# A graph layer on one core: the preamble's loads and searches in another order

## The reference

```python
h_self  = x @ W_self.T + b_self
messages = x[src] @ W_neigh.T + b_neigh
h_neigh = segment_sum(messages, dst, num_segments=50000)
out = layernorm(x + relu(h_self + h_neigh))      # over the 128 features, eps 1e-5
```

## Time and profile before

| | us |
|---|---|
| median of three runs | 803.71 (801.73 to 805.24) |
| profiled execution | 807.21 |
| its span, from the first to the last instruction | 805.3 |
| busy: PE, DVE, POOL, ACT | 548.5, 446.5, 405.0, 303.8 |

### The profile page before, as it was taken

One profiled execution on the slowest core, in us unless ns is written; L12 is line 12 of the kernel. 1 busy time (PEld: TensorE's weight loads), 2 busy tenths in 40 slices (PEclk: granted clock), 3 DMA queues, 4 the chain that ended last, 5 costly groups with the idle time before them and its releaser, 6 DMA issues.

```text
span 805.3 us, 11397 instructions
## 1 busy us (share of the span) xinstructions
PE 548.5 (68%) x3151; PEld 434.5 (54%) x3151; DVE 446.5 (55%) x1927; ACT 303.8 (38%) x789; POOL 405.0 (50%) x424
## 2 busy tenths in 40 slices
PE   1036020118941879889678787888989798999995
PEld 0024010016730657677456576666767576778784
DVE  6783001008821768689566666675645455666765
ACT  0000000015501444446244354435445354566566
POOL 3687777731176556562756566556656566200000
PEclk9999555558985799999879999889979899999998
DMA  4222222113331435444334444434544444433333
GB/s 136 62 63 65 53 52 62 52 27 92 102 83 52 113 103 145 125 129 128 93 93 132 119 122 110 126 110 132 133 110 129 129 126 129 122 109 101 112 107 93
DMA packets 122933, 82.12 MB, mean 102 GB/s; under 512 B 15374, under 2 KB 115894, under 8 KB 122840
## 3 DMA queue, kind: packets, MB, share of 16 engines
q1 hardware_dynamic: 109208, 53.63, 23.5%
q0 software_dynamic: 13664, 27.77, 13.6%
HBM read 55.44 MB, written 26.71 MB: 102 GB/s over the span
## 4 chain that ended last, share of the span: by engine, by line
PE 41%; issue 21%; DVE 15%; another core or an unknown queue 11%; ACT 6%; POOL 4%; DMA 2%; ACTq 1%; DVEq 0%; POOLq 0%
PE bank L889 17%; PE bank L908 8%; PE bank L909 7%; DVE pick L724 4%; PE bank L873 4%; ACT result L1017 3%; PE bank L904 3%; DVE y L735 2%; PE bank L883 2%; DVE stats L755 2%; ACT sums_t L990 1%; POOL ring L462 1%; DMA dst_block<-in_dst,block_index 1%; POOL dst_block L422 1%
## 5 line engine op out<-in xcount | busy, mean ns | idle before, releaser
L462 POOL DMA_INDIRECT ring<-in_x,chunk_src x391 | 379.9, 972 | 265.7 <-issue 110.2
L990 ACT COPY sums_t<-bank 128x496 f32 x131 | 74.9, 572 | 415.5 <-remote 223.1
L889 PE MATMUL bank<-pick,ring 128*128 128x192 f32 (+2 forms) x782 | 227.6, 431 | 2.4 <-DMA ring<-in_x,chunk_src 2.4
L908 PE MATMUL bank<-wsum_t,x_t 128*128 128x128 f32 (+1 forms) x782 | 173.2, 304 | 11.7 <-issue 11.5
L735 DVE SCALAR_TENSOR_TENSOR y<-bank,x_in 128x384 f32<-128x384 f32 x131 | 72.5, 554 | 191.5 <-PE bank L909 73.9
L909 PE MATMUL bank<-wn_t,sums_t 128*128 128x128 f32 (+1 forms) x782 | 158.6, 284 | 19.4 <-issue 19.4
L1017 ACT ACTIVATE result<-y,minus_mean,rstd 128x128 f32<-128x128 f32 x391 | 163.4, 486 | 0.0
L889 PEld LDWEIGHTS bank<-pick,ring 128*128 128x128 f32 x782 | 142.5, 205 | 17.1 <-DMA ring<-in_x,chunk_src 1.9
L908 PEld LDWEIGHTS bank<-wsum_t,x_t 128*128 128x128 f32 (+1 forms) x782 | 124.8, 200 | 37.7 <-issue 37.7
L909 PEld LDWEIGHTS bank<-wn_t,sums_t 128*128 128x128 f32 (+1 forms) x782 | 125.5, 201 | 18.9 <-issue 18.9
L724 DVE TENSOR_SCALAR pick<-columns,local 128x192 f32<-128x192 f32 (+2 forms) x391 | 118.0, 357 | 0.2
(11 more groups left out here) (122 smaller groups left out, 208.8 us busy)
## 6 DMA issues: line engine op xcount, KB each, us to landing
x_in<-in_x SPq DMA_DIRECT2D x130, 192.0 KB
out<-result SPq DMA_DIRECT2D x130, 192.0 KB
ring<-in_x,chunk_src POOLq DMA_INDIRECT x391
degrees_t<-degrees_dram SPq DMA_DIRECT2D x130, 2.2 KB
dst_padded<-in_dst SPq DMA_DIRECT2D x1, 390.6 KB
src_padded<-in_src SPq DMA_DIRECT2D x1, 390.6 KB
edge_src<-in_src SPq DMA_DIRECT2D x1, 390.6 KB
edge_dst<-in_dst SPq DMA_DIRECT2D x1, 390.6 KB
```

The lines of the kernel that those rows point to most:

```text
L462: nc.gpsimd.indirect_dma_start(ring[:, c % RING, :], None, x, bass.IndirectOffsetOnAxis(ap=chunk_src[:, c:c + 1], axis=0)).then_inc(gather ...
L889: ins = mm(sums[:, lo:hi], ring[:, c % RING, :], pick[tau % DEEP][:, PICK_AT[q]:PICK_AT[q] + hi - lo], start=(tau == 0 and q == 0), stop=( ...
L908: mm(h, x_t[b][:, q, 0:rows], k.wsum_t[:], start=False, stop=False)
L990: nc.scalar.copy(sums_t[:, bass.ds(at, SPAN)], sum_bank[tau % SUM_BANKS][:, 0:SPAN]).then_inc(sums_placed, 1)
```

## The change

SP: the four first `x` loads go behind the bias loads, and the bias loads wait for the windows of column 0. The three loads of the edge list for the check move into the main loop, to the step that loads `x` tile trio 37. POOL: all four `dst` blocks of the ranks and the first tile block are fetched before the windows of column 0, the other tile blocks after them; the windows of columns 1 to 3 now go before the tile windows. DVE: the search for tile blocks goes before the search in the first rank block, the last bias parts and the search in rank blocks 1 to 3 go before the packing, and only the tile search is left inside it. Nothing is added to or taken from what is computed, except the wait on `window_landed[0]` on SP.

```diff
--- before.py
+++ after.py
@@ -365,32 +365,36 @@  (sync engine)
+            def load_edges():
+
+                sp.dma_start(edge_src[:], src.rearrange("(p e) -> p e", p=EDGE_ROWS)).then_inc(edges_landed, 16)
+                sp.dma_start(edge_dst[:, 0:EDGE_COLS], dst.rearrange("(p e) -> p e", p=EDGE_ROWS)).then_inc(edges_landed, 16)
+                sp.wait_ge(next_set, 1)
+                sp.dma_start(edge_dst[0:EDGE_ROWS - 1, EDGE_COLS:EDGE_COLS + 1],
+                             dst.rearrange("(p e) -> p e", p=EDGE_ROWS)[1:EDGE_ROWS, 0:1],
+                             allow_slow_non_contiguous=True).then_inc(next_landed, 16)
+
...
-            for tau in range(DEEP):
-                load_x(tau)
-
-            sp.dma_start(edge_src[:], ...
-            sp.dma_start(edge_dst[:, 0:EDGE_COLS], ...
-            sp.wait_ge(next_set, 1)
-            sp.dma_start(edge_dst[0:EDGE_ROWS - 1, EDGE_COLS:EDGE_COLS + 1], ...
-
             sp.wait_ge(k.parts_made, 3)
+            sp.wait_ge(window_landed[0], 32)
             for q in range(TRIO):
                 sp.dma_start(k.bias[q * PARTS:(q + 1) * PARTS, q, :], ...
 
+            for tau in range(DEEP):
+                load_x(tau)
             store_degrees(1, 0, 1)
...
                 if tau == FIRST_TRIOS:
                     store_degrees(2, 1, 2)
+                if tau == FIRST_TRIOS + DEEP:
+                    load_edges()
@@ -440,17 +444,18 @@  (gpsimd)
             pool.wait_ge(blocks_found, 1)
             load_blocks(0, [0])
+            pool.wait_ge(blocks_found, 2)
+            load_blocks(0, range(1, COLUMNS))
+            pool.wait_ge(blocks_found, 3)
+            load_blocks(1, [0])
             pool.wait_ge(padded_stored, 64)
             pool.wait_ge(places_found, 1)
             load_windows([0])
-            pool.wait_ge(blocks_found, 2)
-            load_blocks(0, range(1, COLUMNS))
-            pool.wait_ge(blocks_found, 3)
-            load_blocks(1, range(COLUMNS))
+            load_blocks(1, range(1, COLUMNS))
             pool.wait_ge(places_found, 2)
+            load_windows(range(1, COLUMNS))
+            pool.wait_ge(places_found, 3)
             load_tile_windows(range(COLUMNS))
-            pool.wait_ge(places_found, 3)
-            load_windows(range(1, COLUMNS))
@@ -540,9 +545,9 @@  (vector engine)
             find_blocks(0, 0, 1)
             find_blocks(0, 1, COLUMNS)
-            find_rank_places(0, 1)
             dve.wait_ge(ends_spread, 2)
             find_blocks(1, 0, COLUMNS)
+            find_rank_places(0, 1)
@@ -641,31 +646,30 @@
             v.tensor_copy(k.bias_part[:, 0, :, :], k.bias_row[:]).then_inc(k.parts_made, 1)
 
-            pack_start(0, 1)
-            pack_bits(0, 1, range(0, 3))
-            find_tile_places(0, COLUMNS)
-            pack_bits(0, 1, range(3, 5))
-            find_rank_places(1, COLUMNS)
-            pack_bits(0, 1, range(5, SHIFT_BITS))
-            pack_end(0, 1)
...
-            take_lists(1, 0, 1)
-            spread_lists(1, 0, FIRST_TRIOS, 0, FIRST_TRIOS - 1)
-
             dve.wait_ge(k.parts_made, 1)
             link(v.tensor_tensor(k.bias_rest[:, 0, :, :], k.bias_row[:], k.bias_part[:, 0, :, :], ALU.subtract))
             v.tensor_copy(k.bias_part[:, 1, :, :], k.bias_rest[:, 0, :, :]).then_inc(k.parts_made, 1)
             dve.wait_ge(k.parts_made, 2)
             link(v.tensor_tensor(k.bias_rest[:, 1, :, :], k.bias_rest[:, 0, :, :], k.bias_part[:, 1, :, :], ALU.subtract))
             v.tensor_copy(k.bias_part[:, 2, :, :], k.bias_rest[:, 1, :, :]).then_inc(k.parts_made, 1)
+            find_rank_places(1, COLUMNS)
+
+            pack_start(0, 1)
+            pack_bits(0, 1, range(0, 3))
+            find_tile_places(0, COLUMNS)
+            pack_bits(0, 1, range(3, SHIFT_BITS))
+            pack_end(0, 1)
...
+            take_lists(1, 0, 1)
+            spread_lists(1, 0, FIRST_TRIOS, 0, FIRST_TRIOS - 1)
```

More of the change, by code:

```diff
@@ L371, in store @@
                 sp.dma_start(rows_of(out, tau), result[tau % DEEP][0:rows, 0:tiles, :]).then_inc(stored[tau % DEEP], 16)
-            for tau in range(DEEP):
-                load_x(tau)
-            sp.dma_start(edge_src[:], src.rearrange("(p e) -> p e", p=EDGE_ROWS)).then_inc(edges_landed, 16)
-            sp.dma_start(edge_dst[:, 0:EDGE_COLS], dst.rearrange("(p e) -> p e", p=EDGE_ROWS)).then_inc(edges_landed, 16)
-            sp.wait_ge(next_set, 1)
-            sp.dma_start(edge_dst[0:EDGE_ROWS - 1, EDGE_COLS:EDGE_COLS + 1],
-                         dst.rearrange("(p e) -> p e", p=EDGE_ROWS)[1:EDGE_ROWS, 0:1],
-                         allow_slow_non_contiguous=True).then_inc(next_landed, 16)
             sp.wait_ge(k.parts_made, 3)
+            sp.wait_ge(window_landed[0], 32)
             for q in range(TRIO):
@@ L642, in _ @@
             v.tensor_copy(k.bias_part[:, 0, :, :], k.bias_row[:]).then_inc(k.parts_made, 1)
+            dve.wait_ge(k.parts_made, 1)
+            link(v.tensor_tensor(k.bias_rest[:, 0, :, :], k.bias_row[:], k.bias_part[:, 0, :, :], ALU.subtract))
+            v.tensor_copy(k.bias_part[:, 1, :, :], k.bias_rest[:, 0, :, :]).then_inc(k.parts_made, 1)
+            dve.wait_ge(k.parts_made, 2)
+            link(v.tensor_tensor(k.bias_rest[:, 1, :, :], k.bias_rest[:, 0, :, :], k.bias_part[:, 1, :, :], ALU.subtract))
+            v.tensor_copy(k.bias_part[:, 2, :, :], k.bias_rest[:, 1, :, :]).then_inc(k.parts_made, 1)
+            find_rank_places(1, COLUMNS)
             pack_start(0, 1)
@@ L661, in _ @@
             spread_lists(1, 0, FIRST_TRIOS, 0, FIRST_TRIOS - 1)
[L663 to L668, removed]
             def check_edges():
```

## The result

The changed kernel took **797.0 us** (median of 4 runs, 791.7 to 803.8) where the kernel before took 804.5: a ratio of **0.990, 95% interval 0.986 to 0.995**. The only profiled execution is the slowest of the four, 803.8 us with a span of 802.0, against 807.2 and 805.3 before. The traces thus differ by 3.4 us and the medians by 7.5; what the three faster runs did better no trace shows.

The account below looks back on a forecast made before the run. The preamble was taken to bound the end through the first gather (8.9 us earlier) and PE's start (6.9); other costs 0. The middle, 8 us, takes the profiled 807.2 to 799.2, as a median 796; range 792 to 800, 8 in 10: 784 to 810.

Parts of the forecast that it names:

- First gather 8.9 us earlier, at 38.1: Preamble: POOL and DVE reorderings let the first gather start at 38.1 where it was 46.99, 8.9 us earlier.
- The windows of column 0: POOL's preamble: sign that these windows would go at 16.79 and 18.10, 1.15 us earlier than before.
- DVE no longer waits in the search of tile blocks: DVE's preamble: sign that the tile block search has no waits, taking 1.9 us out of the packing.
- Rival 3: Preamble: the last tile block lands late beside the `x` loads, losing 0 to 1.5 us; 797; chance 0.15.
- PE's start 6.9 us earlier, at 59.7: End of preamble: the first bias product moves from 66.58 to about 59.7, 6.9 us earlier.
- Slow stretch and second list: Main loop: the stretch with hardly a matmul ends near 172, and the second list of gathers begins near 210.
- Rival 1: Slow stretch: it ends for PE's own reason, so the gain is absorbed; 0 to 3 us gained, 802; chance 0.13.
- rival 4: The slow stretch of 105 us turns out shorter, or the second one goes, giving 31 us, about 765; chance 0.10.
- Edge loads at 0, at most 2 to 3 us: Main loop, ahead of trio 37's `x` load: edge loads cost 0, at most one late `x` tile, 2 to 3 us.
- Rival 2: Main loop, pass 33 or so: late edge loads start another slow stretch, 31 us lost less 8 gained, 819; chance 0.14.
- The sum, 8 us, 796: Whole kernel: gathers 8.9 us and PE 6.9 us earlier, the middle taken as 8 us, giving 796.

Follow-up runs that it names:

- e1: Changed kernel with the three edge loads right behind the first four `x` loads instead of at pass 37: 575.33 us, ratio to before 0.9905.
- e2: Changed kernel with a ring of 24 gathered chunks in place of 84: 581.65 us, ratio to before 1.0014.
- e5: Changed kernel, nothing altered, on a later chip: 583.35 us, ratio to the kernel before 1.0044.
- e7: Changed kernel with the three edge loads apart, at passes 37, 41 and 45: 576.03 us, ratio to before 0.9921.
- e8: Changed kernel with the two large edge loads behind the first `x` loads, only the short one at pass 37: 576.15 us, ratio to before 0.9924.
- e9: Changed kernel with edge loads behind the first four `x` loads, plus 24 matmuls nothing reads in pass 0: 573.54 us, ratio to before 0.9883.
- e6: The kernel before, nothing altered, on a later chip: 579.91 us.
- e3: Kernel before with the new SP part alone (edge loads at pass 37), POOL and DVE in the old order: 582.67 us, ratio to before 1.0035.
- e10: Kernel before with the new SP part, but edge loads right behind the first four `x` loads; old POOL and DVE orders: 578.34 us, ratio to before 0.9954.
- e12: Kernel before with the new SP part, but edge loads at passes 37, 41 and 45; old POOL and DVE orders: 579.02 us, ratio to before 0.9975.
- e11: Repeat of the changed kernel with edge loads behind the first four `x` loads: 575.54 us, ratio to before 0.9898.

## Why the prediction was right, and where it was not

- **First gather 8.9 us earlier, at 38.1:** right, 38.36 (and 38.2 to 38.5 in the traces of e1, e2, e5, e7, e8 and e9). The windows of column 0 went at 17.14 and 18.55, forecast 16.79 and 18.10; DVE no longer waits in the search of tile blocks, as the new profile's `dst_block` loads land in 2.6 to 2.8 us. Rival 3, a late last block, didn't come.
- **PE's start 6.9 us earlier, at 59.7:** the time is right, 59.76, but the term is not. I took the first bias product as the end of PE's preamble. From there to the second it is 5.3 to 6.8 us in ten of the twelve traces that have a part of the change, where it is 3.7 in both traces of before, as PE runs at half rate; 128x128 products last 0.42 us (median in e5) for 0.28 (e6). What makes it do so there and not in e3, e6 and e10 is open (e9 above). From pass 1 on, 4.1 us of the 7.2 are left in e5. How much it is changes from trace to trace (3.70 in e3, 5.37 in e12 with the same preamble).
- **Slow stretch and second list:** forecast to end near 172 and to begin near 210; POOL resumes at 170.52 and the list begins at 210.09. So in these two traces the end of the stretch moved with the gathers, as the forecast assumed, and pass 0's loss was repaid: 8.4 us ahead at pass 7, and again at pass 32. That the gathers cause it is not shown by this. Rival 1 (the gain is absorbed) and rival 4 (a shorter stretch) didn't happen.
- **Edge loads at 0, at most 2 to 3 us:** wrong. From bias product 32 to 40 it was 40.64 us where the kernel before took 32.55, so 8.1 us, and 7.2 in e5 against e6, the largest error of the sum. I counted the lead of the `x` loads as four trios of 4.9 us, the mean pace from the earlier trace rows, some 20 us. In fact SP issues the load of trio 37 only when the tile of trio 33 has been used and its queue has come to it, and PE is by then in trio 34 and turns tile 37 ahead of the products of 36. The trace of the kernel before had the true lead, 8.4 us (358.55 to 366.90). With 780 KB ahead the load needs 10.6 us to land in e5 and 12.2 in the first trace. And I had no term for the slower products behind a wait, 3.0 us in e5. Rival 2 named the place, pass 37, with another mechanism and price (a new slow stretch, 31 us); that one was not seen. Its time, 819, takes the gain of 8 us off twice: 31 us lost and 8 gained from 804 are 827.
- **The sum, 8 us, 796:** the medians say 7.5 and 797.0, the two traces say 3.4. By the traces it is 8.4 us at pass 32, less 8.1, and 3.0 won again from pass 40 to 128 beside the gathers, which the sum had no term for. The medians' other 4 us are not explained, and with a term of 8 us left out the hit on the median is in part luck. On the chip of e5, the only other one that ran the change as it was made, the same terms without the slow stretch (7.2 - 3.1 - 7.2 - 1.7 + 0.7 us, the 1.7 not explained) make it 4 us slower in the traces and 0.4% by the medians. That the time of the kernel itself depends so much on the chip was in none of my cases.

**What stays open** is what sets PE's half rate (e9 above), and the slow stretches. These are in both traces of the first runs, of before and after, and in none of the twelve of the four chips later, where gathers also run with hardly a pause (391 from 47.70 to 548.48 in e6, 1.28 us each). So back-to-back gathers are not enough for them; what else that chip or that hour had, no run here shows. Every experiment ran without them, so the 1% that was measured at first has its parts read from two traces, and none of them was tested where it was measured.

**The version that beats both:** the new preamble with the edge loads behind the first `x` loads, 0.990 of before (e1 and e11, on two chips), by the ratios 1.4% under the change as it was made (e5, on a third); with the idle matmuls (e9) 0.988, not told apart from it. It was not run where the kernel takes 804 us.

## What to carry to other kernels

A load that is taken out of the preamble isn't free in the loop. Ask which load stands behind it in the same queue, how long a batch of that size holds it, and how much lead that load has. Read the lead in the trace, from the load's issue to the time when its reader is ready, and don't count it in buffers. Four buffers gave 7.5 us here, two passes. A wait of PE can cost more than its length, 7.2 us for 4.2 here. A large load that nothing needs soon goes best into the part where its queue waits anyway and nothing urgent follows (e1; in e10 the degrees did); if it must go into the loop, one piece for each few passes. And a part that starts PE earlier is worth what PE's second pass shows, since an earlier first product can meet a PE whose clock has fallen while it waited.

## What the runs showed of the hardware that I had not expected

- One program took 804 us in the first runs and 580 on four chips later, with granted clocks of 0.87 and 0.98 to 0.99. A profile from one chip can hide what bounds the kernel on another.
- In e5 the clock row of 59 to 67 us says 1.00, though the 128x128 products in it last 0.42 us (median 421 ns of 7) for the 0.28 of the full rate. The durations told the rate there, the clock row didn't. (In e1, and in e5 at 208 us, the row says 0.50 beside products of the same length.) First the stretch, columns as in the table by stretch:

```profile
59.00:67.00 8.00, 7.11 (x26) 5.66 (x26) 3.54 (x13) 0.55 (x2) 6.00 (x7) 1.00 0.31 75
```

then the products of that stretch (ns min/median/max, first and last start us, shapes):

```profile
L912 PE MATMUL bank<-wsum_t,x_t x7: 377/421/582, 60.3 to 67.0; 128*128 128x128 f32 x7
```
